# A two-layer cross-attention block in one fused kernel: when the later weights are loaded and split, and the order of copies in the first SELF and the last CROSS group

## The chip, the cores and the metric

The kernel runs on one core of a Trainium2 chip. The metric is the device time of one execution in microseconds (us); lower is better. Five engines work side by side, each through its own list of instructions, and meet at semaphores: PE (TensorE, matrix products and transposes through the identity), DVE (VectorE), ACT (ScalarE), POOL (GpSimd) and SP (SyncE, which here only issues DMAs). PEld is the load of a product's stationary operand, which runs beside PE. PE's clock has two levels, 1.2 and 2.4 GHz; the profile gives the granted one as a share of the higher, so 0.50 is 1.2 GHz.

## What is computed

The input x has 32 sequences of 64 rows by 128, the context 32 by 64 by 96. Layer 0 has three blocks, each added to its input; layer 1 has a small cross-attention and a feed-forward block. Cut to what matters:

```python
def _attn(xq, xc, Wq, Wk, Wv, Wo, bo):          # 16 heads of 64
    q, k, v = heads(xq @ Wq), heads(xc @ Wk), heads(xc @ Wv)
    attn = softmax(einsum('bnhd,bshd->bhns', q, k) * 64 ** -0.5)
    return merge(einsum('bhns,bshd->bnhd', attn, v)) @ Wo + bo

x = _attn(_ln(x, g1, b1), _ln(x, g1, b1), Wq1, Wk1, Wv1, Wo1, bo1) + x   # SELF
x = _attn(_ln(x, g2, b2), context, Wq2, Wk2, Wv2, Wo2, bo2) + x          # CROSS
x = (a * gelu(gate)) @ Wf + bf + x      # GEGLU; a, gate = split(_ln(x, g3, b3) @ Wp + bp)
out = _attn8(x, context) @ Wo + bo      # CROSS2; 16 heads of 8, with biases
y = x + out + gelu(_ln(out, g4, b4) @ W1 + b1) @ W2 + b2                 # FFN
```

## The kernel before

**Tiling.** The 2048 rows are 16 tiles of 128, taken two at a time: 8 groups (`GROUPS`) of 256 rows (`GR`), numbered 0 to 7. The program runs through five phases in turn, SELF, CROSS, GEGLU, CROSS2 and FFN, and through all 8 groups in each. `Step(phase, g)` names one group of one phase. In a SELF or CROSS group g ("t" is one of its two tiles) the steps are:

- `x_step` turns the normalised rows `xn` (PE, L598), ACT scales them into `xT` and rounds them to `src0h` or `src1h` (even or odd group); POOL makes the remainder `src0r` or `src1r` (`rest_step`, L1365). A product of full precision is three products of rounded parts (`three`, L583 to L585).
- `proj_step`, called for the group that follows, makes queries and keys in 8 pieces, 0 to 3 for q and 4 to 7 for k. Each piece is six PE products into one of three PSUM banks (`stage`) and is copied out by ACT, pieces 1 and 7 by DVE (`PROJ_BY_DVE`; `p_step` on those engines, L903 and L1135).
- `scores_step` (PE, L670) for t = 0 and 1, then `max_step`, `shift_step` (DVE, L1156 and L1161), `exp_step` (ACT, L959), `sum_step` with a reciprocal (DVE, L1189 and L1191) and the scaling of the probabilities `pr` on POOL (L1420, signals `probs`).
- `val_step` makes the values in four pieces (each copied half by ACT, half by DVE, `vt`, L903 and L1196), `turn_step` transposes the probabilities (PE, L712; copied by ACT and DVE, `pt`), `av_step` multiplies both (PE, L742; copied to `ot`), and `out_step` applies Wo (PE, L761); DVE adds the result to `rows` (L1212, signals `added`).

**What sets the order.** Each engine's list is written by hand in its own `group(s)` function; nothing is scheduled by a tool. `Counts` replays PE's order once to know which count each semaphore has at each step. The three `stage` banks go round: `stage_for` makes PE wait, before it writes a bank, until the copies of the piece three uses earlier are made. The score banks `scp` and the bank `out0p` stand beside them. `keep_warm(bank, n)` writes n products of the identity with itself that nothing reads.

**Around the change.** The SP list (L496 to L517) loads the first rows and the SELF weights, waits for the first exponential (`exped`), and then issues Wo of SELF, the four CROSS weights, 15 small vectors (`VECTORS`), the eight weights of the later phases, and the first context tiles, with no wait between them. The CROSS weights q and k must be split into a rounded part (ACT, `high_step`) and a remainder (POOL, `weight_step`, L1386); this is done at the end of SELF groups 0 and 1 for q and k, and of group 6 for v. Before group 0 there is a hand-written start on each engine: on DVE it splits Wq and Wk of SELF (`rest_step` at L1093), copies pieces 1 and 7 of group 0, and makes the statistics of group 1 (`stats_step`). In the last CROSS group (`last`) there is no next projection; in its place stand the first GEGLU pieces (`p_step(one, ...)`, bank copied by ACT's gelu, L951, and DVE's product, L1150) and a table load for the gelu on ACT (`load_table`).

## Time and profile before

| what | value |
| --- | --- |
| time, median of 3 runs | 477.34 us |
| the three runs | 477.17, 477.34, 480.69 us |
| the profiled execution's own time | 480.08 us |
| its span in the trace | 478.3 us (so 1.8 us lie outside it) |
| mean granted PE clock | 0.989 |
| PE, DVE, ACT, POOL busy | 96%, 75%, 59%, 40% of the span |

All durations come from the one profiled execution, which took 2.7 us more than the median. In a row of the timeline the first number is the start in us from the span's beginning, the second the length of the whole row, and the bracket at the end is the engine's idle time just before it and what ended that. Matmuls overlap, so the distance between starts says more than a length. A row of the waits gives the waiting instruction, the releaser, and then total us, number of times and the longest.

### The profile page before, as it was taken

The numbers are of one execution on the slowest core, as the hardware profiler recorded it, in microseconds if no ns is written. First come the engines' busy times: TensorE is split into PE (matmuls) and PEld (weight loads), VectorE is DVE, ScalarE is ACT, GpSimd is POOL, SyncE is SP. The second block draws the span as 40 slices with busy tenths as digits, with TensorE's granted clock in tenths as the row PEclk, the third lists the DMA queues.
The fourth block names the chain that finished last, engine by engine and source line by source line (L and its number), as shares of the span: only waits on it lengthen the run. The fifth ranks groups of instructions, "written<-read, shape, count | busy, mean of one in ns | idle before, by whom it ended". The sixth has DMA issues, their size and how long they took to land.

```text
span 478.3 us, 17632 instructions
## 1 busy us (share of the span) xinstructions
PE 458.4 (96%) x7640; PEld 416.7 (87%) x7640; DVE 359.9 (75%) x654; ACT 281.6 (59%) x505; POOL 192.9 (40%) x216
## 2 busy tenths in 40 slices
PE   7798999999999999999999999989999999998897
PEld 7687998998989989989899898978999787777797
DVE  4766788887887878778878788796785578688562
ACT  5354665655647665566565664754464667676773
POOL 1734353524433445435452444324342313132473
PEclk9979999999999999999999999998999999999999
DMA  7174000000000000000000000000000000000011
GB/s 224 53 180 146 2 3 3 1 3 3 1 5 1 11 12 1 12 1 11 11 2 12 10 3 11 3 1 3 2 0 8 18 11 18 2 1 3 1 44 45
DMA packets 17300, 10.57 MB, mean 22 GB/s; under 512 B 7888, under 2 KB 16272, under 8 KB 17232
## 3 DMA queue, kind: packets, MB, share of 16 engines
q1 hardware_dynamic: 16800, 9.48, 7.2%
q8 instruction: 56, 0.92, 0.9%
q10 hardware_dynamic: 432, 0.07, 0.1%
q14 instruction: 12, 0.10, 0.1%
HBM read 8.50 MB, written 1.05 MB: 20 GB/s over the span
## 4 chain that ended last, share of the span: by engine, by line
PE 83%; DVE 10%; issue 2%; ACT 2%; DMA 1%; POOL 1%; DVEq 0%; SPq 0%
PE out0p L761 12%; PE stage L583 12%; PE stage L584 11%; PE stage L585 11%; PE stage L742 7%; PE scp L670 7%; PE scp L712 6%; PE scp L882 6%; DVE mx L1166 3%; PE out0p L777 2%; PE scp L686 2%; DVE vb L1143 1%; PE stage L795 1%; DVE pr L1161 1%; DMA pr<-in_L_xattn_Wq_dram 1%
## 5 line engine op out<-in xcount | busy, mean ns | idle before, releaser
L1420 POOL TENSOR_TENSOR pr<-pr,rc 128x1024 f32<-128x1024 f32 x32 | 60.9, 1902 | 95.3 <-DVE rc L1191 95.2
L761 PE MATMUL out0p<-wo_of,ot 128*128 128x128 f32 x512 | 68.1, 282 | 0.0
L761 PEld LDWEIGHTS out0p<-wo_of,ot 128*128 128x128 f32 x512 | 60.8, 192 | 2.1
L959 ACT ACTIVATE pr<-pr 128x1024 f32<-128x1024 f32 x48 | 50.6, 1054 | 16.9 <-DVE pr L1161 14.3
L903 ACT ACTIVATE q_of_heads<-stage 128x512 f32<-128x512 f32 x48 | 28.5, 595 | 49.3 <-PE stage L585 47.4
L903 ACT ACTIVATE vt<-stage 64x512 f32<-64x512 f32 x64 | 37.8, 591 | 27.6 <-PE stage L585 26.0
L1196 DVE COPY vt<-stage 64x512 f32<-64x512 f32 x64 | 44.4, 693 | 4.0 <-PE stage L585 1.1
L1189 DVE TENSOR_REDUCE sm<-pr 128x16 f32<-128x1024 f32 x32 | 38.9, 1216 | 7.9 <-ACT pr L959 7.9
L1156 DVE TENSOR_REDUCE mx<-scp 128x16 f32<-128x1024 f32 x32 | 38.2, 1195 | 6.9 <-PE scp L670 6.9
L742 PE MATMUL stage<-pt,vt 64*64 64x64 f32 x2048 | 38.1, 224 | 2.3 <-issue 2.3
L670 PEld LDWEIGHTS scp<-k_of_heads,q_of_heads 64*64 64x64 f32 x2048 | 33.2, 134 | 8.0 <-ACT ot L903 5.5
L1161 DVE TENSOR_TENSOR pr<-scp,mx 128x1024 f32<-128x1024 f32 x32 | 39.2, 1225 | 1.1
L742 PEld LDWEIGHTS stage<-pt,vt 64*64 64x64 f32 x2048 | 33.6, 137 | 7.2 <-issue 2.7
L670 PE MATMUL scp<-k_of_heads,q_of_heads 64*64 64x64 f32 x2048 | 37.8, 221 | 0.1
L1338 POOL TENSOR_TENSOR rstd<-veps,neghalf 128x2 f32<-128x2 f32 x32 | 22.7, 710 | 35.8 <-DVE veps L1109 35.7
L712 PEld LDWEIGHTS scp<-ident,pr 128*128 128x128 f32 x256 | 30.5, 143 | 4.5 <-POOL pr L1420 0.4
L712 PE MATMUL scp<-ident,pr 128*128 128x128 f32 x256 | 34.1, 277 | 0.2 <-POOL pr L1420 0.2
L903 ACT ACTIVATE k_of_heads<-stage 128x512 f32<-128x512 f32 x48 | 28.7, 597 | 7.2 <-PE stage L585 1.6
L1399 POOL TENSOR_TENSOR masked_k<-kT,fourmask 128x1024 f32<-128x1024 f32 x8 | 15.1, 1893 | 43.8 <-ACT kT L940 43.8
L1365 POOL TENSOR_TENSOR src0r<-xT,src0h 128x256 fp32r<-128x256 f32 x16 | 11.7, 730 | 49.2 <-ACT src0h L903 28.3
L1200 DVE COPY ot<-stage 128x512 f32<-128x512 f32 x32 | 22.1, 690 | 11.2 <-PE stage L742 10.4
L1365 POOL TENSOR_TENSOR src1r<-xT,src1h 128x256 fp32r<-128x256 f32 x16 | 11.7, 729 | 46.0 <-ACT src1h L903 25.1
(235 smaller groups left out, 1277.9 us busy)
## 6 DMA issues: line engine op xcount, KB each, us to landing
ctx_in<-in_ctx_dram SPq DMA_DIRECT2D x16, 96.0 KB, 2.0
wo_of<-in_L_xattn_Wo_dram SPq DMA_DIRECT2D x2, 512.0 KB, 6.1
out_dram<-rows SPq DMA_DIRECT2D x8, 128.0 KB, 1.8
rows<-in_x_dram SPq DMA_DIRECT2D x1, 768.0 KB, 9.4
pr<-in_L_xattn_Wq_dram SPq DMA_DIRECT2D x1, 512.0 KB, 4.8
pr<-in_L_xattn_Wk_dram SPq DMA_DIRECT2D x1, 512.0 KB, 6.2
pt<-in_L_xattn_Wv_dram SPq DMA_DIRECT2D x1, 512.0 KB, 7.6
rows<-in_L_xattn_Wq_dram SPq DMA_DIRECT2D x1, 512.0 KB, 5.6
```

Of the source, the lines that this page charges most:

```text
L583: nc.tensor.matmul(dst, wh, mh, start=start, stop=False)
L584: nc.tensor.matmul(dst, wh, mr, start=False, stop=False)
L585: return nc.tensor.matmul(dst, wr, mh, start=False, stop=True)
L670: last = nc.tensor.matmul(scp[64 * b:64 * b + 64, 2 * t + e, a * N:(a + 1) * N], heads_of[0][h, a, n], heads_of[1][h, a, n], start=True, s ...
L712: last = nc.tensor.transpose(scp[:, 2 * t + c, q * 128:(q + 1) * 128], pr[t][:, a * 128:(a + 1) * 128], ident[:, :])
L742: last = nc.tensor.matmul(banks[i][64 * e:64 * e + 64, m * ROWS + b * N:m * ROWS + (b + 1) * N], vt[h, 2 * t + b, (2 * m + e) * DH:(2 * m ...
L761: last = nc.tensor.matmul(out0p[:, t * D:(t + 1) * D], ot[:, a // 2, a % 2, t, :], wo_w[s.phase][:, a, :], start=(a == 0), stop=(a == PAIR ...
L903: return nc.scalar.activation(dst, s, ACT.Copy)
L959: nc.scalar.activation(pr[t][:, :], pr[t][:, :], ACT.Exp, scale=scale[s.phase]).then_inc(exped, 1)
L1161: nc.vector.tensor_tensor(halves(pr[t][:, :]), sc3, mx[:, t, :, None].to_broadcast([ROWS, H, N]), ALU.subtract).then_inc(shifted, 1)
L1196: nc.vector.tensor_copy(*value_copy(s, u, 1)).then_inc(dve, 1)
L1420: nc.gpsimd.tensor_tensor(halves(pr[t][:, :]), halves(pr[t][:, :]), rc[:, t, :, None].to_broadcast([ROWS, H, N]), ALU.mult).then_inc(probs, 1)
```

## The change

On SP, every later load gets a wait of its own (`pace(g, t)` waits for the exponential of SELF group g, tile t): after Wo of SELF the CROSS weights q, k, v, o wait for (1,0), (1,1), (2,0), (2,1), the 15 vectors for (3,0), and Wp, W1, Wf, W2 for (3,1), (4,0), (4,1), (5,0); the four small weights and the first context tiles follow behind. The splits of CROSS Wq and Wk move from the ends of SELF groups 0 and 1 to those of groups 3 and 4 on ACT and POOL. In SELF group 0, ACT copies piece 0 of the next projection ahead of the first exponential, and DVE copies piece 1 right behind the first shift. In the start, DVE makes the statistics of group 1 before it copies piece 1 and splits Wk, and POOL makes the remainder of group 1 before two bias additions. In the last CROSS group, DVE copies value piece 1 and makes the second sum ahead of the addition to `rows` and the statistics; and PE, ahead of the second `turn_step`, waits for `shifted` of tile 1 and runs five products of the identity into `scp[:, 2, :]`, which nothing reads.

```diff
--- before.py
+++ after.py
@@ -499,17 +499,27 @@
             load_rows(T, T, loaded_rows[1])
             load_weight(SELF, "v")
             load_rows(2 * T, TILES - 2 * T, loaded_rows[2])
-            sp.wait_ge(exped, cnt.at("exp", Step(SELF, 0), 0))
+
+            def pace(g, t=0):
+
+                sp.wait_ge(exped, cnt.at("exp", Step(SELF, g), t))
+
+            pace(0)
             load_weight(SELF, "o")
-            for key in "qkvo":
+            for n, key in enumerate("qkvo"):
+                pace(1 + n // 2, n % 2)
                 load_weight(CROSS, key)
+            pace(3)
             for dst, name in VECTORS.items():
                 load_vector(sp, dst, name, loaded_small)
-            for dst, s in ((wp[:, :], w["L0_xattn_Wp"]), (w1[:, :], w["L1_xattn_W1"]),
-                           (wf[:, :, :], w["L0_xattn_Wf"].rearrange("(a p) d -> p a d", p=128)),
-                           (w2[:, :, :], w["L1_xattn_W2"].rearrange("(a p) d -> p a d", p=128)),
-                           (wq1[:, :], w["L1_xattn_Wq"]), (wk1[:, :], w["L1_xattn_Wk"]),
-                           (wv1[:, :], w["L1_xattn_Wv"]), (wo1[:, :], w["L1_xattn_Wo"])):
+            for n, (dst, s) in enumerate((
+                    (wp[:, :], w["L0_xattn_Wp"]), (w1[:, :], w["L1_xattn_W1"]),
+                    (wf[:, :, :], w["L0_xattn_Wf"].rearrange("(a p) d -> p a d", p=128)),
+                    (w2[:, :, :], w["L1_xattn_W2"].rearrange("(a p) d -> p a d", p=128)),
+                    (wq1[:, :], w["L1_xattn_Wq"]), (wk1[:, :], w["L1_xattn_Wk"]),
+                    (wv1[:, :], w["L1_xattn_Wv"]), (wo1[:, :], w["L1_xattn_Wo"]))):
+                if n < 4:
+                    pace(3 + (n + 1) // 2, (n + 1) % 2)
                 sp.dma_start(dst, s).then_inc(loaded_ffn, 16)
             c = w["ctx_768"].rearrange("b n d -> (b n) d").rearrange("(t p) d -> p t d", p=ROWS)
 
@@ -705,6 +715,9 @@
 
             def turn_step(s, t):
 
+                if s.is_group(CROSS, GROUPS - 1) and t == 1:
+                    pe.wait_ge(shifted, cnt.at("shifted", s, t))
+                    keep_warm(scp[:, 2 * t, :], 5)
                 pe.wait_ge(probs, cnt.at("probs", s, t))
                 for c in range(2):
                     for q in range(4):
@@ -999,6 +1012,8 @@
                 one, two = s.ahead(1), s.ahead(2)
                 if s.phase in (SELF, CROSS):
                     before, last = s.before(), one.phase == GEGLU
+                    if not before:
+                        p_step(one, (0,))
                     exp_step(s, 0)
                     if before:
                         av_step(before, 1)
@@ -1012,7 +1027,8 @@
                         pt_step(s, 0)
                         p_step(one, (1,))
                     else:
-                        p_step(one, (0,))
+                        if before:
+                            p_step(one, (0,))
                         exp_step(s, 1)
                         p_step(one, range(1, 8))
                         val_step(s, (0, 1))
@@ -1024,9 +1040,9 @@
                     if last:
                         p_step(one, (2, 3))
                     x_step(two)
-                    if s.is_group(SELF, 0):
+                    if s.is_group(SELF, 3):
                         high_step(CROSS, "q", high_cross)
-                    if s.is_group(SELF, 1):
+                    if s.is_group(SELF, 4):
                         high_step(CROSS, "k", high_cross)
                     if s.is_group(SELF, GROUPS - 2):
                         high_step(CROSS, "v", high_cross)
@@ -1230,22 +1246,26 @@
                     shift_step(s, 0)
                     if before:
                         av_step(before, 1)
+                    else:
+                        p_step(one, range(4))
                     sum_step(s, 0)
                     max_step(s, 1)
                     shift_step(s, 1)
                     if last:
-                        val_step(s, (0,))
-                    else:
+                        val_step(s, (0, 1))
+                        sum_step(s, 1)
+                    elif before:
                         p_step(one, range(4))
                     if before:
                         out_step(before)
                     if s.is_group(SELF, 0):
                         ve.wait_ge(loaded_rows[2], 16)
                     stats_step(two)
-                    sum_step(s, 1)
                     if last:
-                        val_step(s, (1,))
                         p_step(one, (0,))
+                    else:
+                        sum_step(s, 1)
+                    if last:
                         val_step(s, (2,))
                         pt_step(s, 0)
                         p_step(one, (1,))
@@ -1310,13 +1330,12 @@
             for c in range(2):
                 ve.wait_ge(high_self, 1 + c)
                 rest_step("q", c, 2)
+            ve.wait_ge(loaded_rows[1], 16)
+            stats_step(Step(SELF, 1))
+            p_step(Step(SELF, 0), range(4))
             for c in range(2):
                 ve.wait_ge(high_self, 3 + c)
                 rest_step("k", c, 2)
-                if c == 0:
-                    p_step(Step(SELF, 0), range(4))
-            ve.wait_ge(loaded_rows[1], 16)
-            stats_step(Step(SELF, 1))
             ve.wait_ge(loaded_w[SELF]["v"], 16)
             nc.vector.tensor_copy(wv_s[SELF][0][:, :], raw[SELF]["v"]).then_inc(high_v, 1)
             p_step(Step(SELF, 0), range(4, 8))
@@ -1423,7 +1442,7 @@
                     norm_step(two, one)
                     bias_step(two)
                     rest_step(two)
-                    for n, (key, first) in enumerate((("q", 0), ("k", 1), ("v", GROUPS - 2))):
+                    for n, (key, first) in enumerate((("q", 3), ("k", 4), ("v", GROUPS - 2))):
                         if s.is_group(SELF, first):
                             weight_step(key, n + 1)
                     for n in range(2):
@@ -1451,9 +1470,9 @@
             rest_step(Step(SELF, 0))
             rstd_step(Step(SELF, 1))
             norm_step(Step(SELF, 1), Step(SELF, 0))
+            rest_step(Step(SELF, 1))
             for g in range(2):
                 bias_step(Step(SELF, g))
-            rest_step(Step(SELF, 1))
             nc.gpsimd.memset(headmask[:, :], 1.0).then_inc(made_mask, 1)
             gp.wait_ge(made_mask, 1)
             nc.gpsimd.affine_select(out=headmask[:, :], in_=headmask[:, :], compare_op=ALU.is_ge, fill=0.0, base=0,
```

The orders follow as the built programs have them. Line numbers differ between the two kernels: L903, L959, L1135, L1156, L1161, L1189, L1191 of before are L916, L972, L1151, L1172, L1177, L1205, L1207 of the change. First ACT, from the end of the start into SELF group 0; `pr` is the exponential, `q_of_heads` the copies of pieces 0, 2 and 3. Before:

```order
14 L903 ACTIVATE src1h<-xT 128x256
15 L959 ACTIVATE pr<-pr 128x1024
16 L903 ACTIVATE q_of_heads<-stage 128x512
17 L959 ACTIVATE pr<-pr 128x1024
18 L903 ACTIVATE q_of_heads<-stage 128x512 x2
```

After:

```order
14 L916 ACTIVATE src1h<-xT 128x256
15 L916 ACTIVATE q_of_heads<-stage 128x512
16 L972 ACTIVATE pr<-pr 128x1024 x2
17 L916 ACTIVATE q_of_heads<-stage 128x512 x2
18 L916 ACTIVATE k_of_heads<-stage 128x512 x3
```

The copy of piece 0 now stands ahead of both exponentials; the copies of pieces 2 and 3 still stand behind both.

Then DVE in SELF group 0, from the first maximum to the statistics of group 2. Before:

```order
17 L1156 TENSOR_REDUCE mx<-scp 128x16
18 L1161 TENSOR_TENSOR pr<-scp,mx 128x1024
19 L1189 TENSOR_REDUCE sm<-pr 128x16
20 L1191 RECIPROCAL rc<-sm 128x16
21 L1156 TENSOR_REDUCE mx<-scp 128x16
22 L1161 TENSOR_TENSOR pr<-scp,mx 128x1024
23 L1135 COPY q_of_heads<-stage 128x512
24 L1100 BN_STATS stats<-rows 128x6 x2
```

After:

```order
16 L1172 TENSOR_REDUCE mx<-scp 128x16
17 L1177 TENSOR_TENSOR pr<-scp,mx 128x1024
18 L1151 COPY q_of_heads<-stage 128x512
19 L1205 TENSOR_REDUCE sm<-pr 128x16
20 L1207 RECIPROCAL rc<-sm 128x16
21 L1172 TENSOR_REDUCE mx<-scp 128x16
22 L1177 TENSOR_TENSOR pr<-scp,mx 128x1024
23 L1116 BN_STATS stats<-rows 128x6 x2
```

The copy of piece 1 moved up by four instructions.

Last, DVE in the last CROSS group, behind the second shift (`vt` are halves of value pieces, `hid` the first GEGLU product, `rows` the addition of the previous group's output). Before:

```order
351 L1161 TENSOR_TENSOR pr<-scp,mx 128x1024
352 L1196 COPY vt<-stage 64x512
353 L1212 TENSOR_TENSOR rows<-out0p,rows 128x256
354 L1100 BN_STATS stats<-rows 128x6 x2
...
357 L1109 TENSOR_SCALAR veps<-mv 128x2
358 L1189 TENSOR_REDUCE sm<-pr 128x16
359 L1191 RECIPROCAL rc<-sm 128x16
360 L1196 COPY vt<-stage 64x512
361 L1150 SCALAR_TENSOR_TENSOR hid<-stage,cols,ge 128x256
362 L1196 COPY vt<-stage 64x512
363 L1205 COPY pt<-scp 128x512
```

After:

```order
350 L1177 TENSOR_TENSOR pr<-scp,mx 128x1024
351 L1212 COPY vt<-stage 64x512 x2
352 L1205 TENSOR_REDUCE sm<-pr 128x16
353 L1207 RECIPROCAL rc<-sm 128x16
354 L1228 TENSOR_TENSOR rows<-out0p,rows 128x256
355 L1116 BN_STATS stats<-rows 128x6 x2
...
358 L1125 TENSOR_SCALAR veps<-mv 128x2
359 L1166 SCALAR_TENSOR_TENSOR hid<-stage,cols,ge 128x256
360 L1212 COPY vt<-stage 64x512
361 L1221 COPY pt<-scp 128x512
```

The second value copy, the second sum and its reciprocal moved ahead of the addition and the statistics; the copy of `pt` has the same instructions before it as it had.

## Rows read from the trace of the kernel before

**Rows 1.** The page: busy time, and granted PE clock in 40 slices of the span.

```profile
PE 458.4 (96%) x7640; PEld 416.7 (87%) x7640; DVE 359.9 (75%) x654; ACT 281.6 (59%) x505; POOL 192.9 (40%) x216
...
PEclk9979999999999999999999999998999999999999
```

**Rows 2.** Waits of PE, whole span: total us, times, longest.

```profile
PE stage L583 <- DVE q_of_heads L1135: 3.0, 1, 3.0
PE stage L742 <- issue: 2.3, 1, 2.3
PE stage L583 <- DVE vt L1196: 1.7, 1, 1.7
```

**Rows 3.** Timeline of PE, SELF group 0: start, length, instruction, idle before and releaser.

```profile
18.29 0.38 PE L583 MATMUL stage<-src1h,wq_of0h 128*128 128x256 f32 x1 [0.50 <-POOL src1r L1365]
...
25.03 0.58 PE L583 MATMUL stage<-src1h,wk_of0h 128*128 128x256 f32 x1 [3.02 <-DVE q_of_heads L1135]
...
30.32 0.59 PE L583 MATMUL stage<-wv_of0h,src0h 128*128 128x512 f32 x1
```

**Rows 4.** Timeline of ACT, SELF group 0: the two exponentials and the copies between.

```profile
19.44 1.06 ACT L959 ACTIVATE pr<-pr 128x1024 f32<-128x1024 f32 x1 [2.62 <-DVE pr L1161]
...
24.41 1.06 ACT L959 ACTIVATE pr<-pr 128x1024 f32<-128x1024 f32 x1 [3.43 <-DVE pr L1161]
25.38 1.06 ACT L903 ACTIVATE q_of_heads<-stage 128x512 f32<-128x512 f32 x2
```

**Rows 5.** Windows: length, busy PE, PEld, DVE, ACT, POOL (count), clock, DMA share, GB/s.

```profile
24.00:25.00 1.00, 0.00 (x0) 0.00 (x0) 1.00 (x3) 0.59 (x1) 0.11 (x1) 0.50 1.06 431
...
30.00:31.00 1.00, 1.00 (x6) 0.87 (x6) 0.44 (x1) 0.00 (x0) 0.81 (x2) 0.63 0.98 19
```

**Rows 6.** Timeline of PE, SELF group 1, around the wait put down to issue.

```profile
41.98 0.46 PE L742 MATMUL stage<-pt,vt 64*64 64x64 f32 x15 [2.25 <-issue]
```

**Rows 7.** DMA queues in the window 39.5 to 40.0: packets, MB, share.

```profile
q8 instruction: 1, 0.02, 12.0%
```

**Rows 8.** Timeline of SP: the first and the last small vector.

```profile
22.99 1.08 SPq L474 DMA_DIRECT2D cols<-in_L_xattn_g_dram  x1
...
32.49 0.43 SPq L476 DMA_DIRECT2D bias<-in_L_xattn_b_dram  x1
```

**Rows 9.** Timeline of ACT, first exponential of SELF group 3.

```profile
81.01 1.06 ACT L959 ACTIVATE pr<-pr 128x1024 f32<-128x1024 f32 x1 [1.17 <-DVE pr L1161]
```

**Rows 10.** Timeline of DVE, last CROSS group.

```profile
318.75 0.69 DVE L1196 COPY vt<-stage 64x512 f32<-64x512 f32 x1
...
320.74 1.21 DVE L1189 TENSOR_REDUCE sm<-pr 128x16 f32<-128x1024 f32 x1
...
324.23 0.69 DVE L1205 COPY pt<-scp 128x512 f32<-128x512 f32 x1
```

**Rows 11.** Timeline of ACT, last CROSS group: copy of value piece 1.

```profile
320.02 0.59 ACT L903 ACTIVATE vt<-stage 64x512 f32<-64x512 f32 x1
```

**Rows 12.** Timeline of POOL, last CROSS group: the second scaling.

```profile
322.32 1.90 POOL L1420 TENSOR_TENSOR pr<-pr,rc 128x1024 f32<-128x1024 f32 x1 [3.96 <-DVE rc L1191]
```

**Rows 13.** Timeline of PE, last CROSS group.

```profile
320.36 1.04 PE L712 MATMUL scp<-ident,pr 128*128 128x128 f32 x8
323.11 0.36 PE L583 MATMUL stage<-src0h,wp_h 128*128 128x256 f32 x1 [1.71 <-DVE vt L1196]
...
324.27 1.97 PE L712 MATMUL scp<-ident,pr 128*128 128x128 f32 x8 [0.21 <-POOL pr L1420]
326.17 1.83 PE L742 MATMUL stage<-pt,vt 64*64 64x64 f32 x64
```

**Rows 14.** Timeline of PE, SELF group 2: the same two steps at clock 1.00.

```profile
74.31 1.04 PE L712 MATMUL scp<-ident,pr 128*128 128x128 f32 x8
75.28 1.16 PE L742 MATMUL stage<-pt,vt 64*64 64x64 f32 x64
```

**Rows 15.** Window with the transposes and products of rows 13; columns as in rows 5.

```profile
324.00:328.00 4.00, 3.79 (x74) 3.33 (x73) 1.98 (x4) 1.07 (x2) 2.83 (x5) 0.57 0.03 6
```

## The prediction, made before the changed kernel was run

> **What bounds the kernel.** I read the page first. PE is busy 96% of the span (the table ahead), and its clock row stands at 9 with dips only in slices 3 and 28 [rows 1]; so PE sets the end, and a change can gain only where PE waits or runs at the lower clock. The waits of PE, longest first, name the places [rows 2]: 3.0 us for a DVE copy, 2.3 us put down to "issue" (nothing in the profile releases it), 1.7 us for another DVE copy. Each occurs once, and each lies where the change works: SELF group 0, SELF group 1, last CROSS group. The list has no other wait of 0.3 us or more in SELF and CROSS behind the start, so from 46 to 321 us PE runs through, and what is saved ahead of that stretch arrives at the end whole.
>
> **SELF group 0.** PE starts the next projection at 18.29 after 0.50 us for POOL's remainder, and stands before piece 4 until 25.03 after 3.02 us [rows 3]. Piece 4 takes the bank of piece 1, which DVE copies only behind the second shift. The second thing to see is the price after the wait: in the window 24 to 25 the granted clock is 0.50, and it is back only in the window 30 to 31 [rows 5]; pieces 4 to 7, 24 products, take 30.32 - 25.03 = 5.29 us [rows 3], 0.22 us each.
>
> What the change does here: piece 1 is copied behind the first shift (done when the first exponential starts, 19.44 [rows 4]), piece 0 by ACT ahead of that exponential. Both banks come free by about 20.1. POOL makes the remainder before its two bias additions, which removes most of the 0.50 us. So PE goes through pieces 0 to 4 without the wait and stands at about 21.3. What is late next: piece 5 takes the bank of piece 2, and ACT copies that behind the second exponential, which neither starts earlier (its chain, first exponential, sum, maximum, shift, is as long as before) nor is passed by the copy. The second exponential starts at 24.41, the pair of copies behind it at 25.38 [rows 4]; half of that pair's 1.06 us makes 25.9, so PE resumes at about 26.0 with pieces 5 to 7. The wait is not removed but moved by one piece, from 3.0 to about 4.7 us. At the lower clock 18 products take 18 x 0.22 = 4.0 us and end at 30.0, against 30.32. The clock then comes back somewhere during the values. I take **-0.3 us**. Bounds: at the higher clock at once the 18 products would take half of 4.0 us and end at 28.0: -2.3 us; if the lower clock lasts as long after resuming as it did here (to 30.65 + 1.0), the first values also run at half rate and it comes to +0.3 us. The reordered start costs nothing I can find: the Wk remainder may reach piece 4 of group 0 some 0.1 us late, and it is behind the same copy.
>
> **SELF group 1 and the loads.** The wait of 2.25 us ends at 41.98 in the middle of 64 products that need no further semaphore (49 ran before it, 15 after) [rows 6]. PE has nothing to wait for but its own instructions. In the half microsecond from 39.5 the queues show one packet of the instruction queue q8 [rows 7]; between 20 and 39.5 the view of the queues shows none, while SP's unpaced loads were in flight, the small vectors from 22.99 to 32.9 and the big FFN weights behind them [rows 8]. In the rest of SELF and CROSS, with almost nothing in flight, such packets come every few microseconds and PE never waits for "issue". I read it as instructions that arrive late behind the loads. In the change only Wo of SELF is in flight then, and the first paced load leaves at about 41: **-2.25 us**. Bounds: 0, if the wait has another cause, and -2.25. On DMA contention as its cause there is a rule against me: the Trainium skill (Runtime: NRT & Kernel Launch, "Instruction fetch mechanics") says that instruction fetch is mostly hidden, since the sequencer dispatches slower than the instruction memory fills. The rows hold a wait of 2.25 us there, so here it was not hidden at least once; by the rule alone this term would be 0 and the sum 477.9.
>
> What the paced loads add: five are released by the first exponential of a group (CROSS q, v, the vectors, W1, W2), at 81.01 + 1.06 in group 3 [rows 9] and some 20 us before and after in the others, and three by the second. Their data land one or more microseconds later, while PE is in the projection, which issues few instructions per microsecond. The vectors take 10 us to issue [rows 8], which pushes Wp to about 93, close to the transposes of group 3. Nobody waits for the data: the first user is the split at the end of group 3, and the last context tile leaves at about 122, well before CROSS. I take 0 for a load, with 2.25 us as the bound if one makes the fetch late again.
>
> The splits moved to groups 3 and 4 cost ACT 1.04 us each between `src` and the exponential. There ACT idles 1.17 us [rows 9], so it fits; without that cover the exponential would be 1.0 us late, and since PE asks for the probabilities much later, still 0.
>
> **Last CROSS group.** PE stands 1.71 us before the second GEGLU piece, since that takes the bank of value piece 1, whose DVE half stands behind the addition, the statistics and the second sum [rows 10, 13]. Then the transposes of tile 1 wait for POOL, 324.27, and the clock falls: the window 324 to 328 has 0.57 [rows 15]. Transposes take 1.97 instead of 1.04 us and products 1.83 instead of 1.16 [rows 13, 14]: 0.93 + 0.67 = 1.6 us. In the change DVE makes both value copies from 318.75 (0.72 each) and then the sum at about 320.2 instead of 320.74 [rows 10]. ACT's half is done at 320.02 + 0.59 = 320.6 [rows 11], before the first transposes end at about 321.3 [rows 13], so the 1.71 us go. POOL starts 0.55 to 0.6 us earlier than 322.32 [rows 12] and ends at about 323.65. PE would finish the GEGLU piece at about 322.2 (it takes 324.06 - 323.11 = 0.95 us [rows 13]), run the five unread products (0.12 us each by the eight transposes of 0.97 us start to start [rows 14]) to 322.8 and wait 0.9 us: about half of the former gaps of 1.71 + 0.21. I take it that the clock stays up. Then the transposes run from 323.7 to 324.6; the products need DVE's `pt`, which has the same work ahead of it as before and ends at 324.23 + 0.69 = 324.9 [rows 10]. This is what is late next. They run from 325.0 to 326.1, against 326.17 + 1.76 = 327.9 [rows 13]: **-1.9 us**. Bounds: with the clock falling all the same, 323.7 + 1.9 + 1.76 = 327.4, -0.6 us; with `pt` no limit, -2.3 us. The five products fill a wait, so they cost 0.
>
> **Sum.** 480.08 - 0.3 - 2.25 - 1.9 = 475.6 us, against the profiled execution's own time. But that one is 2.7 us above the median 477.34, and its size is that of one of these accidents. If the two executions at 477.2 had no late fetch, the change brings them only 0.3 + 1.9, to 475.1; if they had no fallen clock in CROSS, 2.25 + 0.3 and about 0.3 of the last term, to 474.5. The middle of the three is **475.2 us**, 0.45% below the median.
>
> **Rivals.**
> The issue wait stays. For it: it is one event, and the packet lies in 39.5 to 40.0, two microseconds before the wait ends [rows 6, 7]. Against it: it is the only one in 16 SELF and CROSS groups with the same instructions, and at the one place with full queues. The other two terms alone give 477.9 from this execution, and about 477.3 if the wait comes and goes with the run. 0.17.
>
> The clock still falls in CROSS, or stays low longer in group 0 (PE is idle 1.7 us longer there than before). For it: a pause of 1.71 us sufficed once, while the 2.25 us of rows 6 did not. The gain shrinks by 1.3 us or 0.6 us: 476.2 to 477.0. 0.14.
>
> The clock comes back early in group 0, up to 1.8 us more: 473.4 to 474.3. For it: the fallen stretch is shorter by six products; against it, the longer idle time. 0.10.
>
> Slower: the paced loads make the fetches late in steady SELF, where nothing hides it. Each release by a first exponential falls into the stretch of products and scores, which eats instructions fastest. Five at 2.25 us are 11.25, less 2.2 for the two other terms and 2.25 for the old one: 480.08 + 6.8 = 486.9. With two late fetches it evens out, 480.1 - 4.45 + 4.5; from three it is slower than before. Against it: each load is 512 KB or less, against about 4 MB in a row. 0.04.
>
> The forecast itself, 474.4 to 476.1: 0.55.
>
> **Range and chances.** The range 473.4 to 477.6 takes in the early clock, both failed terms and the median of before itself, and leaves out late fetches in number. A change of about 1% (4.8 us) is what a measurement here can tell from none. Faster by that (under 472.6) needs group 0 at the higher clock and both other gains in full: 0.06. Slower (over 482.1) needs four late fetches: 0.03. Same: 0.91.
>
> **What would show it.** Right: PE's list of waits has no "issue" wait of 2 us near 40; the wait of group 0 stands before a `k_of_heads` piece near 26 and names ACT; the window at 323 to 327 of before (some 3 us earlier) has clock 1.00, with transposes of 1.04 and products of 1.16 us; the wait of 1.71 us is gone and one of about 0.9 us stands after five products of the identity. Wrong: an "issue" wait at one of the paced loads; a clock of 0.50 past 32 us; an exponential in groups 4 or 5 that waits for a split; a time over 477.6 or under 473.4.

## The result, and the profile after

The changed kernel takes 475.49 us in the median of 20 runs (474.25 to 476.33), the kernel before 477.38 in 20 runs (475.38 to 483.13). The ratio is 0.9946, 95% interval 0.9927 to 0.9964: half a per cent faster, as forecast (475.2 us, 0.45%). Of the three gains that the forecast was added up from only that of the loads was right; the two others brought nothing in the medians, and that the number came out all the same is luck, as told further down. The profiled execution after took 476.33 us with a span of 474.6 (before 480.08 and 478.3).

The page's clock row after, against [rows 1]: the dip in slice 28 is gone, that in slice 3 is as deep.

```profile
PEclk9979999999999999999999999999999999999999
```

The longest waits of PE after, against [rows 2]:

```profile
PE stage L593 <- ACT q_of_heads L916: 4.2, 1, 4.2
...
PE stage L755 <- DVE pt L1221: 0.9, 1, 0.9
...
PE scp L725 <- POOL pr L1439: 0.5, 1, 0.5
```

The three old waits (DVE copy 3.0, issue 2.3, value copy 1.7) are gone. A longer one, for an ACT copy, stands in SELF group 0, and two short ones in the last CROSS group. PE's timeline at the first, against [rows 3], with the first row of the values after it:

```profile
26.11 0.58 PE L593 MATMUL stage<-src1h,wk_of0h 128*128 128x256 f32 x1 [4.21 <-ACT q_of_heads L916]
...
30.12 0.63 PE L593 MATMUL stage<-wv_of0h,src0h 128*128 128x512 f32 x1
...
32.14 1.04 PE L725 MATMUL scp<-ident,pr 128*128 128x128 f32 x8
```

And the windows there, to be read with [rows 5] (the clock is the first number behind POOL's bracket):

```profile
30.00:31.00 1.00, 1.00 (x5) 0.81 (x5) 0.64 (x1) 0.00 (x0) 0.92 (x2) 0.50 0.00 0
31.00:32.00 1.00, 1.00 (x5) 0.82 (x4) 0.41 (x2) 0.36 (x1) 0.92 (x2) 0.75 0.00 0
```

PE is 0.2 us ahead of [rows 3] when it reaches the values (30.12 against 30.32), but the clock comes back a microsecond later than before, and the first transposes start at 32.14, where they started at 31.89. PE in SELF group 1, against [rows 6]: all 64 products in one row, no wait.

```profile
39.02 1.16 PE L755 MATMUL stage<-pt,vt 64*64 64x64 f32 x64
40.11 1.16 PE L774 MATMUL out0p<-wo_of,ot 128*128 128x128 f32 x8
```

The last CROSS group after, PE, then DVE, then POOL, against [rows 10, 12, 13]:

```profile
317.78 1.04 PE L725 MATMUL scp<-ident,pr 128*128 128x128 f32 x8
...
319.37 1.28 PE L588 MATMUL scp<-ident 128*128 128x128 f32 x10
321.16 1.09 PE L725 MATMUL scp<-ident,pr 128*128 128x128 f32 x8 [0.52 <-POOL pr L1439]
323.11 1.16 PE L755 MATMUL stage<-pt,vt 64*64 64x64 f32 x64 [0.86 <-DVE pt L1221]
```

```profile
317.62 1.22 DVE L1205 TENSOR_REDUCE sm<-pr 128x16 f32<-128x1024 f32 x1
...
320.36 0.78 DVE L1125 TENSOR_SCALAR veps<-mv 128x2 f32<-128x2 f32 x1
...
322.27 0.69 DVE L1221 COPY pt<-scp 128x512 f32<-128x512 f32 x1
```

```profile
319.21 1.90 POOL L1439 TENSOR_TENSOR pr<-pr,rc 128x1024 f32<-128x1024 f32 x1 [3.42 <-DVE rc L1207]
```

The five unread products are the row of ten at 319.37, 1.28 us long: such a product is two rows of the trace, where a transpose is one. Transposes and products run at the full clock. But `pt` still holds PE back, for 0.86 us.

**Where the 3.7 us of the two profiles went**, from starts of PE rows: to the first transposes +0.25 (31.89 to 32.14); from there to the second scores of group 1, 11.57 us before (to 43.46) and 9.06 after (to 41.20), -2.51; from there to the last scores of CROSS (314.57, 311.99) -0.32 over 270 us, which I did not trace further (e1, e2, e4 to e10 take 270.1 to 270.9 us for this stretch, so part of it may be mere variation); from those to the last feed-forward product (471.80, 468.11) 157.23 before and 156.12 after, -1.11.

### The profile page after: what moved, and what is told of

It reads as the page before. It is cut to its first block, busy times and chain, and to the rows that moved or that the text cites. A ratio compares the mean times of both kernels' runs of the same rounds, so it can differ in the third digit from the quotient of the medians.

```text
span 474.6 us, 17652 instructions
## 1 busy us (share of the span) xinstructions
PE 457.4 (96%) x7650; PEld 416.3 (88%) x7650; DVE 361.2 (76%) x654; ACT 281.6 (59%) x505; POOL 193.2 (41%) x216
## 4 chain that ended last, share of the span: by engine, by line
PE 84%; DVE 10%; ACT 2%; issue 2%; POOL 1%; DMA 1%; DVEq 0%; ACTq 0%; POOLq 0%
PE out0p L774 13%; PE stage L593 12%; PE stage L594 11%; PE stage L595 11%; PE stage L755 7%; PE scp L680 7%; PE scp L725 6%; PE scp L895 6%; DVE mx L1182 3%; PE out0p L790 2%; PE scp L696 2%; DVE vb L1159 1%; PE stage L608 1%; PE stage L808 1%; DVE pr L1177 1%
## 5 line engine op out<-in xcount | busy, mean ns | idle before, releaser
L972 ACT ACTIVATE pr<-pr 128x1024 f32<-128x1024 f32 x48 | 50.7, 1056 | 14.8 <-DVE pr L1177 12.2
L916 ACT ACTIVATE q_of_heads<-stage 128x512 f32<-128x512 f32 x48 | 28.4, 595 | 50.7 <-PE stage L595 49.0
L916 ACT ACTIVATE vt<-stage 64x512 f32<-64x512 f32 x64 | 37.9, 592 | 28.1 <-PE stage L595 26.5
L1205 DVE TENSOR_REDUCE sm<-pr 128x16 f32<-128x1024 f32 x32 | 38.9, 1217 | 7.9 <-ACT pr L972 7.9
L1172 DVE TENSOR_REDUCE mx<-scp 128x16 f32<-128x1024 f32 x32 | 38.2, 1195 | 6.7 <-PE scp L680 6.7
L1177 DVE TENSOR_TENSOR pr<-scp,mx 128x1024 f32<-128x1024 f32 x32 | 39.2, 1224 | 1.1
L916 ACT ACTIVATE k_of_heads<-stage 128x512 f32<-128x512 f32 x48 | 28.7, 597 | 7.2 <-PE stage L595 1.8
L916 ACT ACTIVATE ot<-stage 128x512 f32<-128x512 f32 x32 | 18.8, 589 | 16.4 <-PE stage L755 16.4
```

Of the source, the lines that this page charges most:

```text
L916: return nc.scalar.activation(dst, s, ACT.Copy)
L972: nc.scalar.activation(pr[t][:, :], pr[t][:, :], ACT.Exp, scale=scale[s.phase]).then_inc(exped, 1)
L1177: nc.vector.tensor_tensor(halves(pr[t][:, :]), sc3, mx[:, t, :, None].to_broadcast([ROWS, H, N]), ALU.subtract).then_inc(shifted, 1)
```

## The experiments

Table of all of them; "before" ran beside each, with medians of 477.4 to 478.8. "Transposes" is the start of the first transposes of SELF group 0; "tail" the distance from the last scores of CROSS to the last feed-forward product.

| kernel | median us (runs) | lowest to highest | transposes | longest issue wait of PE | tail |
| --- | --- | --- | --- | --- | --- |
| before | 477.38 (20) | 475.4 to 483.1 | 31.89 | 2.25 | 157.23 |
| changed | 475.49 (20) | 474.3 to 476.3 | 32.14 | none | 156.12 |
| e1 loads only | 474.82 (12) | 474.0 to 477.1 | 30.73 | none | 155.73 |
| e2 first group only | 477.57 (12) | 475.2 to 481.7 | 32.04 | 2.02 | 155.70 |
| e3 last group only | 478.96 (12) | 476.1 to 481.7 | 30.85 | 2.76 | 156.09 |
| e4 unpaced | 477.40 (12) | 475.8 to 481.5 | 31.00 | 2.00 | 156.06 |
| e5 no products | 474.77 (10) | 474.3 to 478.5 | 30.83 | none | 156.11 |
| e6 burst later | 475.46 (10) | 474.4 to 476.3 | 30.99 | none | 156.09 |
| e7 copies first | 472.89 (6) | 471.8 to 473.0 | 25.22 | 0.2 (elsewhere) | 156.12 |
| e8 pt first | 474.25 (11) | 473.4 to 475.5 | 31.13 | none | 155.21 |
| e9 both | 470.59 (6) | 470.2 to 471.2 | 26.01 | none | 155.19 |
| e10 CROSS at once | 475.51 (12) | 474.4 to 476.1 | 30.91 | none | 156.10 |
| e11 burst at group 1 | 478.18 (10) | 477.1 to 480.6 | 32.06 | 1.34 | 156.10 |

**e1, e2, e3: one part of the change alone.** e1 takes the paced loads and the later splits into the kernel before:

```diff
-            for key in "qkvo":
-                load_weight(CROSS, key)
+            for n, key in enumerate("qkvo"):
+                pace(1 + n // 2, n % 2)
+                load_weight(CROSS, key)
...
```

> Before, with only the paced loads and the CROSS splits moved to groups 3 and 4. Theory (instructions arrive late behind the loads in flight): PE has no issue wait near 40 us, the profile's span is 2 to 3 us shorter than that of before, the median of the timed runs is 1 to 2 us lower (near 476), and the runs lie within 2.5 us of each other instead of 8. Rival (the issue wait has another cause, the place in the program): the wait of about 2 us is there, median 477.4 and the wide spread stay.

e2 takes only the new order of the start and of SELF group 0 on ACT, DVE and POOL:

```diff
+                    if not before:
+                        p_step(one, (0,))
                     exp_step(s, 0)
...
```

> Before, with only the changed start and SELF group 0 (copies of pieces 0 and 1 earlier, statistics and POOL remainder earlier). Theory (the wait only moves from piece 4 to piece 5): PE waits some 4.2 us before piece 5 for ACT, the first transposes start within 0.3 us of 31.9, and the median stays within 0.5 us of before. Rival (the reorder gains): first transposes at 31.0 or earlier, about 1 us less.

e3 takes only the last CROSS group, on DVE and PE:

```diff
-                        val_step(s, (0,))
+                        val_step(s, (0, 1))
+                        sum_step(s, 1)
...
+                if s.is_group(CROSS, GROUPS - 1) and t == 1:
+                    pe.wait_ge(shifted, cnt.at("shifted", s, t))
+                    keep_warm(scp[:, 2 * t, :], 5)
```

> Before, with only the last CROSS group changed (second sum earlier, five unread products). Theory: clock 1.00 throughout, and 1.1 to 1.2 us less from the scores of the last CROSS group to the end, as in the changed kernel; median near 476.2. Rival (clock falls without the other parts too): 0.5 us less or nothing.

Measured: e1 has the whole gain (ratio 0.9945, 0.9914 to 0.9975), e2 none (1.0013, 0.9979 to 1.0047), e3 none (1.0011, 0.9977 to 1.0046). e1 met its theory on the wait; its median gained more than expected (2.8 us against the 477.63 of before beside it), and its runs spread a little wider (3.0 us). e2 met its theory: the wait moved (4.43 us, for ACT) and the time stayed. e3 missed its: with the old order the tail is 155.7 when the clock stays up, as it does in the profiles of e1 and e2, and with the new order 156.1. So the new order costs 0.4 us; the profile of before is the only one of this study's in which the clock fell there. Here is e1, with the old order and the old wait of 1.7 us, and the transposes nevertheless at full rate:

```profile
318.59 0.36 PE L592 MATMUL stage<-src0h,wp_h 128*128 128x256 f32 x1 [1.72 <-DVE vt L1205]
...
319.76 1.09 PE L721 MATMUL scp<-ident,pr 128*128 128x128 f32 x8 [0.22 <-POOL pr L1429]
320.78 1.16 PE L751 MATMUL stage<-pt,vt 64*64 64x64 f32 x64
```

The profile of e3 shows one thing more. Its wait for instructions is the longest, and the clock fell behind it: the window 43 to 44, with the columns of the windows above, has 0.50, and the scores of group 1 take 1.99 us instead of 1.16.

```profile
41.45 0.46 PE L745 MATMUL stage<-pt,vt 64*64 64x64 f32 x15 [2.76 <-issue]
41.83 1.45 PE L764 MATMUL out0p<-wo_of,ot 128*128 128x128 f32 x8
43.22 1.99 PE L670 MATMUL scp<-k_of_heads,q_of_heads 64*64 64x64 f32 x64
```

```profile
43.00:44.00 1.00, 1.00 (x30) 0.79 (x32) 0.96 (x2) 0.00 (x0) 0.00 (x0) 0.50 0.29 65
```

From the restart to the next projection it is 5.87 us (41.45 to 47.32), against 4.38 in before (41.98 to 46.36) and e4. So the late instructions cost 2.76 us and another 1.5 us of low clock there. This can be why the runs with unpaced loads spread so far; only this one profile shows it.

**e4: the change without the pacing**, splits staying late.

```diff
-            for n, key in enumerate("qkvo"):
-                pace(1 + n // 2, n % 2)
+            for key in "qkvo":
                 load_weight(CROSS, key)
...
```

> The changed kernel with the loads unpaced again as in before, the splits staying in groups 3 and 4. Theory (loads in flight delay instructions): an issue wait near 39 to 42 us in some executions, median 1 to 2 us above the changed kernel (476.5 to 477.5), spread of 4 us or more. Rival (the splits of group 0 on ACT and POOL were the cause, or the place in the program): as the changed kernel, 475.5 with a spread of 2 us.

The gain is gone (1.0003, 0.9971 to 1.0034), and the wait is back before the same 15 products as in [rows 6]:

```profile
37.88 0.97 PE L746 MATMUL stage<-pt,vt 64*64 64x64 f32 x49
40.84 0.46 PE L746 MATMUL stage<-pt,vt 64*64 64x64 f32 x15 [2.00 <-issue]
```

So it is the loads, and not where the splits stand on ACT and POOL. The view of the queues, asked in windows of 0.2 us, gives the start of each packet of the instruction queue q8. Measured from the first transposes, the packet that this place needs comes 4.3 us behind them in e1 (35.0), 4.5 in e10 (35.4) and 4.7 in the changed kernel (36.8), where nothing is in flight; it comes 7.7 behind them in before (39.6), 7.4 in e2 (39.4) and e4 (38.4) and 8.2 in e3 (39.0). It is 3 to 4 us late, and PE starts again 2.4 to 2.5 us behind it in all four. The data queue beside the packet of [rows 7] is nearly full:

```profile
q1 hardware_dynamic: 270, 0.13, 91.0%
```

**e6 and e11: all loads at once, at another time.** e6 releases them by the second exponential of group 1:

```diff
-            pace(0)
+            sp.wait_ge(exped, cnt.at("exp", Step(SELF, 0), 0))
             load_weight(SELF, "o")
+            sp.wait_ge(exped, cnt.at("exp", Step(SELF, 1), 1))
+            for key in "qkvo":
+                load_weight(CROSS, key)
...
```

> The changed kernel with all loads behind Wo of SELF released at once by the second exponential of group 1 (near 46 us), without pacing. Theory (loads in flight delay instructions, wherever they are): the issue wait leaves the place near 40 us and one of 1 to 3 us stands 18 to 22 us later, in the same products of group 2, median 1 to 2 us above the changed kernel. Rival (only the place near 40 us, where the program's first instructions end, is sensitive): no issue wait anywhere, 475.5.

My theory missed here: no issue wait anywhere, and the time of the changed kernel. But the packets show that half of it held. The one that comes at 58.2 in e1 and 59.8 in the changed kernel (both some 27.5 us behind the first transposes) comes at 62.2, in this window, beside full queues:

```profile
q1 hardware_dynamic: 135, 0.18, 97.6%
q8 instruction: 1, 0.02, 11.7%
```

It is 3.6 us late and costs nothing: PE is then in the projection, where a row of PE starts every 0.12 us. The one before it, at 54.6, had been on time, with the data queue at 5.7% in its window of 0.2 us. e11 aims the loads at that one: they are released by the first exponential of group 1, three vectors behind the rest, so that the feed-forward weights go out from 51.66.

```diff
+            sp.wait_ge(exped, cnt.at("exp", Step(SELF, 1), 0))
+            for key in "qkvo":
+                load_weight(CROSS, key)
+            for dst, name in list(VECTORS.items())[:-3]:
+                load_vector(sp, dst, name, loaded_small)
...
```

> The changed kernel with all loads behind Wo of SELF released at once by the first exponential of group 1, so that the feed-forward weights are in flight near 55 us, when the instruction packet for the products at 58 is due (in the changed kernel it came at 55.8); the last three vectors go behind. Theory (a packet that is late costs where its instructions are used soon): packet 2 to 3 us late, an issue wait of 1 to 3 us near 59, median 1 to 2 us above the changed kernel. Rival (only the first such place is sensitive): packet late or not, no issue wait, 475.5.

The packet and the wait met the theory: the packet came at 58.2 instead of 55.7, and PE waited, one group later than before and in the same products:

```profile
58.11 1.15 PE L749 MATMUL stage<-pt,vt 64*64 64x64 f32 x61
60.60 0.33 PE L749 MATMUL stage<-pt,vt 64*64 64x64 f32 x3 [1.34 <-issue]
```

The median is that of before again (1.0001, 0.9971 to 1.0031). That is 2.7 us above the changed kernel, twice the wait and more than the 1 to 2 us expected; the profiled execution alone, at 477.46, is 2.0 us above it. Where the rest is lost I did not trace. So neither the loads alone nor the place alone costs: the packets that fell among the large loads (in before, e2, e3, e4, e6 and e11) came late, and that costs where the instructions are needed at once, in the 64x64 products, whose rows start every 17 ns (64 in 1.09 us, 39.02 to 40.11 in the rows of the changed kernel above).

**e10: only the CROSS weights at once.**

```diff
-                pace(1 + n // 2, n % 2)
                 load_weight(CROSS, key)
```

> The changed kernel with the four CROSS weights released together with Wo of SELF, the vectors and the feed-forward weights still paced. Theory (what counts is what is in flight when the instruction packet is due, some 4.3 us behind the first transposes of group 0, near 35 to 37 us): the five large loads are through by 32, the packet comes on time, no issue wait, median as the changed kernel, 474.5 to 475.5. Rival (any unpaced load costs): issue wait near 40, 476.5 or more.

As the theory had it (0.9938, 0.9914 to 0.9962), level with the changed kernel: five loads of 0.4 to 0.5 MB are through when the packet is due. What the pacing must keep away is the vectors and the feed-forward weights; which of the two does the harm, many small packets or many bytes, no run tells apart.

**e5: the change without the five products and their wait.**

```diff
-                if s.is_group(CROSS, GROUPS - 1) and t == 1:
-                    pe.wait_ge(shifted, cnt.at("shifted", s, t))
-                    keep_warm(scp[:, 2 * t, :], 5)
```

> The changed kernel without the five unread products and without the wait for shifted ahead of them. After the first experiments I expect no difference: with the old order of the last CROSS group and a wait of 1.7 us the clock fell in one profile and stayed up in two, and here the pause is about 1.9 us between busy stretches. Distance from the last scores of the last CROSS group to the last feed-forward product within 0.1 us of the changed kernel's 156.1 if the clock stays, 1.6 us more if it falls. Rival (the products matter): the clock falls in the window 320 to 325, median 1 us or more above 475.5.

No difference in the tail (156.11) nor in the median; PE waits 1.62 us for POOL in one piece and the clock stays up in the profile. But two of its ten runs took 478.3 and 478.5, which no run of the changed kernel did, and the mean granted clock on record for these two is 0.986, against 0.993 or 0.996 for the other eight. So PE ran longer at the lower clock in them. e1, with the old order and no products, has the same: three of its twelve runs show 0.989 and took 476.1 to 477.1, the other nine 0.993 or 0.996 and 474.0 to 475.6. Of the 53 runs of the changed kernel, e6, e8 and e10, which have the products and no issue wait in their profiles, none is below 0.993. Five of 22 against none of 53 speaks for the rival: the products do seem to hold the clock up in the executions in which it would fall, too few for a median to see. The profile of before, at 0.989, is one such execution, with the clock fallen in this place. That the products prevent it is not shown: no slow run of e1 or e5 was traced, and e1 differs from the changed kernel in more than the products.

**e7: what is late next in SELF group 0.**

```diff
-                        if before:
-                            p_step(one, (0,))
+                        p_step(one, (0,) if before else range(1, 8))
                         exp_step(s, 1)
-                        p_step(one, range(1, 8))
+                        if before:
+                            p_step(one, range(1, 8))
...
                     if s.is_group(SELF, 0):
+                        p_step(one, range(4, 8))
                         ve.wait_ge(loaded_rows[2], 16)
```

> The changed kernel, in SELF group 0 with all of ACT's projection copies ahead of the second exponential and DVE's copy of piece 7 behind the second shift. Theory (the banks held behind the exponential cost the 4.2 us): PE has no wait in the eight pieces, runs the values and the first transposes by about 26 and waits for the scaled probabilities of tile 1 until about 29.1; second transposes at 29 to 30 instead of 33.7, 3.5 to 4.5 us less, median near 471.5. Rival (the chain of exponentials gets longer by the copies ahead of it): the second exponential starts after 25.5 and less than 2 us is gained.

Met in the waits, but not in the size: 2.6 us below the changed kernel, where 3.5 to 4.5 were expected; ratio to before 0.9881 (0.9838 to 0.9925). I had reckoned from the profile of the changed kernel, in which the clock came back late; from that of e6, in which it came back early, the span is 2.2 us shorter (472.8 to 470.6). The eight pieces run through, the page's clock row is 9 in all 40 slices, and the second exponential starts at 24.66, near the 24.52 of the changed kernel in spite of the copies ahead of it:

```profile
21.87 2.04 ACT L916 ACTIVATE k_of_heads<-stage 128x512 f32<-128x512 f32 x3
24.66 1.06 ACT L972 ACTIVATE pr<-pr 128x1024 f32<-128x1024 f32 x1 [0.75 <-DVE pr L1177]
```

PE's second transposes then wait for POOL's scaling, as expected:

```profile
29.60 1.09 PE L725 MATMUL scp<-ident,pr 128*128 128x128 f32 x8 [2.65 <-POOL pr L1441]
```

**e8: what is late next in the last CROSS group.**

```diff
+                    if last:
+                        pt_step(s, 0)
+                        p_step(one, (0,))
+                        val_step(s, (2,))
                     if before:
                         out_step(before)
...
                     stats_step(two)
...
```

> The changed kernel, in the last CROSS group with DVE's pt copy, the first GEGLU product and value piece 2 ahead of the addition and the statistics. Theory (the statistics, and the 0.78 us of their last instruction beside POOL, hold pt back): the wait of 0.86 us before the products behind the second transposes goes, and the distance from the last scores to the last feed-forward product falls from 156.1 to 155.2. Rival (the statistics, now later, hold back the next group): unchanged or longer. The median, 0.9 us less, is at the edge of what the runs can tell.

Met in the profile: the tail is 155.21, and PE goes from the transposes into the products without a wait:

```profile
319.73 1.09 PE L725 MATMUL scp<-ident,pr 128*128 128x128 f32 x8 [0.52 <-POOL pr L1439]
320.75 1.16 PE L755 MATMUL stage<-pt,vt 64*64 64x64 f32 x64
```

DVE's `veps` now runs when POOL is idle, and takes 0.17 us again:

```profile
320.94 0.17 DVE L1125 TENSOR_SCALAR veps<-mv 128x2 f32<-128x2 f32 x1
```

The medians point the same way: 474.25 against 475.49 for the changed kernel, and against 475.46 for e6, which is level with it and was timed beside the same runs of before as e8.

**e9: both, and the second maximum and shift ahead of the first sum.**

```diff
+                        p_step(one, (0,) if before else range(1, 5))
                         exp_step(s, 1)
+                        p_step(one, range(1, 8) if before else range(5, 8))
...
+                    if before:
+                        sum_step(s, 0)
                     max_step(s, 1)
                     shift_step(s, 1)
+                    if not before:
+                        sum_step(s, 0)
+                        sum_step(s, 1)
+                        p_step(one, range(4, 8))
```

> The changed kernel with both finds together: in SELF group 0 ACT copies pieces 0, 2, 3, 4 ahead of the second exponential, DVE makes the second maximum and shift ahead of the first sum, and the last CROSS group has the pt copy ahead of addition and statistics. Theory: the second transposes of group 0 start near 28.3 instead of 29.6, clock 1.00 throughout, and 0.9 us less in the last CROSS group; median 470.5 to 471.2. Rival (POOL's two scalings, 1.9 us each, now follow each other and set the time): second transposes not before 29.6, median 472.0.

The best version, as its theory had it: 470.59 us, ratio to before 0.9834 (0.9794 to 0.9874), 4.9 us below the changed kernel. The second transposes start at 27.87. What is late there now is `pt` on DVE, which PE waits for before the products:

```profile
30.16 1.16 PE L755 MATMUL stage<-pt,vt 64*64 64x64 f32 x64 [1.19 <-DVE pt L1220]
```

It is the same thing as in the last CROSS group of the changed kernel. The statistics now stand beside POOL's two scalings, and DVE's `veps` takes 1.29 us and ends with them (27.84 and 27.81). To put the statistics of group 0 behind the `pt` copy, as e8 does in CROSS, is the next step; it was not run.

```profile
26.55 1.29 DVE L1124 TENSOR_SCALAR veps<-mv 128x2 f32<-128x2 f32 x1
```

```profile
24.05 3.76 POOL L1444 TENSOR_TENSOR pr<-pr,rc 128x1024 f32<-128x1024 f32 x2 [2.47 <-DVE rc L1206]
```

## Why the prediction was right, and where it was not

**The issue wait (-2.25).** Right in mechanism and size: -2.51 between the profiles, gone with the pacing, back without it. What failed is the step behind it, "if the two executions at 477.2 had no late fetch". Without pacing all four profiles have the wait (before, e2, e3, e4: 2.0 to 2.8 us), and e1 gains 0.55% in the ratio, about 2.6 us. The timed runs say the same, though less surely, as they have no traces: at one mean granted clock, 0.996, all eleven runs of before beside e1 took longer (474.8 to 475.9) than all six of e1 (474.0 to 474.7), by 1.4 us in the median. So the loads seem to cost something in every execution, and in these less than the wait in the profiles. The runs with unpaced loads spread over 5 to 8 us, where those of the changed kernel spread over 2. As for the rule of the Trainium skill that instruction fetch is mostly hidden (Runtime: NRT & Kernel Launch, "Instruction fetch mechanics"): here it holds in every profile with the loads paced (no issue wait over 0.2 us), and fails in before, e2, e3, e4 and e11; 1.3 to 2.8 us of PE time stood behind one packet.

**The paced loads (0).** Right. No issue wait stands at any of the nine releases. The rival of late fetches in steady SELF did not come; e6 shows a late packet that is harmless in the projection, and e11 that such a wait does come with all loads at once at a bad time.

**SELF group 0 (-0.3).** The mechanism was right: the wait moved to piece 5, PE resumed at 26.11 (forecast 26.0), reached the values at 30.12 (forecast 30.0), and the clock settles the rest. The sign was off: +0.25 between the profiles, within the bounds. The transposes start at one of two levels: 30.7 to 30.9 or 31.9 with the old order (e1 and e3, before), 30.8 to 31.1 or 32.0 to 32.1 with the new (e4, e5, e6, e8 and e10; the changed kernel, e2 and e11). Which one an execution gets depends on when the clock comes back; the new order costs about 0.2 us at either level, in the means of these few profiles. What holds the transposes back are the copies behind the second exponential, as e7 shows.

**The last CROSS group (-1.9).** Two steps failed. First, 1.6 us of the term was the fallen clock, which I took for the old order's price in every execution; in the profiles of e1 and e2 the same order and the same wait pass at full clock, and the clocks of the timed runs (at e5) put it at about one execution in four or five. The third of my three cases had named this and taken 0.3 us for it. Second, that DVE's `pt` "has the same work ahead of it as before" counted instructions and not what runs beside them: with the sum moved up, POOL's scaling (319.21 to 321.11) covers DVE's `veps`, which took 0.78 us instead of 0.17 and ended with it at 321.14. So `pt` ended at 322.96 (322.27 + 0.69), 0.6 us later than reckoned, and at full clock the new order is 0.4 us slower than the old. The five products took 1.28 us and not 0.6, which cost nothing, since POOL was later still. The Trainium skill states a rule that I had left out (SBUF — State Buffer, "SBUF: two separate sides", on the port pair that VectorE and GpSimd share: GpSimd and certain VectorE instructions, those in a two-port mode or with two inputs in SBUF, lock it for a whole instruction, and the other waits). That `veps` is one of them no run shows by itself, but its three long rows agree: each ends within 0.03 us of the POOL instruction beside it (0.78 us here, 1.29 us in e9, and 0.45 us at 326.11 in e8 beside one on 128x256), and in e8 it takes 0.17 us where POOL is idle.

**The sum.** The number came out by luck. The middle one of my three cases, 475.1 (I wrote 475.2), has no late packet in it and takes all of its 2.2 us from the two terms that brought nothing in the medians (e2, e3). The measured 1.9 us between the medians, 2.6 us by the ratio, come from the late packet instead (e1). Of the chances, the 0.91 for no change that can be told from none came: the interval of the ratio ends at a gain of 0.73%, short of 1%.

## What to carry to other kernels

A wait put down to "issue" in the middle of products that need no semaphore is a reason to look at the instruction queue's packets and at what SP has in flight then. Release loads that nobody needs yet by a semaphore of the steady stage, so that they are not in flight when the packet is due that feeds a run of small products; when that is, the queue view shows. Before a copy is moved ahead, follow the ring of banks to the end: here one bank was freed and the next stood behind the same exponential, and all copies ahead of it were worth 2.6 us. And a fallen clock in one profile is not the price of an order in every execution: the mean granted clock of each timed run says how often it falls.

## What I had not expected of the hardware

An instruction packet of 16 KB (56 packets and 0.92 MB on the page of the changed kernel) came 2.5 to 4 us late beside loads (q1 at 91.0% and 97.6%), and a wait of PE (1.3 to 2.8 us) followed only where PE used up its instructions fast. With the same order of instructions, a pause of 1.7 us was once followed by the lower clock (in before) and twice not (e1, e2); one of 2.25 us [rows 6] was not, and one of 2.76 us at the same place was (e3). A DVE instruction on 128x2 elements took 0.78 and 1.29 us beside POOL instructions on 128x1024, and 0.17 us alone.
